# A graph layer with a sort on one core: the compare and exchange stage in six narrow instructions, turned weights in SBUF, and an eleventh gather slot

## The reference

```python
# x: 8192 x 512; src, dst: 131072 node numbers; edge_weight: 131072
h   = layernorm(x) @ L0_gnn_weight.T                    # 8192 x 512
x   = x + segment_sum(edge_weight[:, None] * h[dst], src, 8192)
y   = layernorm(x)
# small network on a few columns of y: nibbles of columns 64..112 by argmax(> 0.5),
# seven layers of 160 x 160, result rounded to 0..15, one-hot, times a mask
x   = x + (y + 2 * one_hots in columns 128..160)
```

## Time and profile before

| | |
|---|---|
| median of three runs | 1762.64 us (1757.96 to 1767.19) |
| profiled execution | 1770.79 us, its span 1768.9 us |
| TensorE (PE), busy | 1601.1 us, 91% |
| VectorE (DVE), busy | 1099.5 us, 62% |
| ScalarE (ACT), busy | 604.3 us, 34% |
| GpSimd (POOL), busy | 1093.6 us, 62% |
| granted TensorE clock | 0.978 of full speed over the span |

### The profile page before, as it was taken

The page is one execution under the profiler, slowest core; times in us unless marked ns, Lnnn a source line. Parts: engine busy times, 40 slices in busy tenths (PEclk is TensorE's granted clock), DMA queues, the critical chain, the costliest instruction groups (busy, mean ns, idle before and its releaser), DMA issues.

```text
span 1768.9 us, 28755 instructions
## 1 busy us (share of the span) xinstructions
PE 1601.1 (91%) x4076; PEld 661.9 (37%) x4077; DVE 1099.5 (62%) x4047; ACT 604.3 (34%) x1354; POOL 1093.6 (62%) x1114
## 2 busy tenths in 40 slices
PE   7999997999989989989998999999999999995995
PEld 4555543333333333333332333333333333332442
DVE  7666575667666876777668766767633333335465
ACT  7777632222222222222222222222234444443341
POOL 1000005777777777777777777777777777775930
PEclk9999998999999999999999999999999999997798
DMA  7333215777777777766776777777777777772334
GB/s 258 116 136 135 89 68 166 206 204 203 200 199 206 201 201 204 202 196 197 201 201 197 206 203 207 201 205 203 206 209 209 208 209 210 208 210 59 132 111 140
DMA packets 121761, 323.87 MB, mean 183 GB/s; under 512 B 20434, under 2 KB 39154, under 8 KB 121586
## 3 DMA queue, kind: packets, MB, share of 16 engines
q0 software_dynamic: 81920, 268.50, 53.4%
q1 hardware_dynamic: 39666, 53.48, 8.8%
HBM read 288.35 MB, written 33.55 MB: 182 GB/s over the span
## 4 chain that ended last, share of the span: by engine, by line
PE 51%; DMA 15%; DVE 13%; POOL 9%; issue 8%; DVEq 3%; ACT 1%; SPq 1%; ACTq 0%
PE psum L1220 30%; DMA region<-h_rows,region 14%; PE psum L1127 12%; POOL region L531 9%; PE psum L1299 4%; DVE region L937 3%; DVE region L846 2%; PE psum L1116 2%; DVEq L937 2%; DVE region L832 2%; DVE region L838 1%; DVE region L840 1%; DVE region L844 1%; PE psum L1267 1%; PE psum L1137 1%
## 5 line engine op out<-in xcount | busy, mean ns | idle before, releaser
L531 POOL DMA_INDIRECT region<-h_rows,region x1024 | 1013.0, 989 | 579.9 <-DMA h_rows<-region 268.1
L1220 PE MATMUL psum<-region 128*128 x2552 | 1204.9, 611 | 109.4 <-DVE region L937 56.3
L1220 PEld LDWEIGHTS psum<-region 128*128 128x128 f32 x2552 | 443.8, 189 | 832.2 <-issue 822.2
L937 DVE SCALAR_TENSOR_TENSOR region<-region 128x128 f32 (+1 forms) x1276 | 444.9, 351 | 388.3 <-PE psum L1220 269.2
L691 ACT ACTIVATE x<-psum 128x512 f32<-128x512 f32 x192 | 114.7, 597 | 772.5 <-PE psum L1220 772.5
L1127 PE MATMUL psum<-region 128*128 128x512 f32 x512 | 230.2, 593 | 0.9 <-ACT region L593 0.9
L846 DVE COPY_PREDICATED region<-region 128x256 f32<-128x256 int32 x407 | 179.5, 441 | 0.0
L674 ACT ACTIVATE psum<-x 128x512 f32<-128x512 f32 x256 | 153.7, 601 | 8.1
L832 DVE TENSOR_TENSOR region<-region 128x128 int32<-128x128 f32 x452 | 128.9, 285 | 24.9 <-ACT region L620 23.4
L844 DVE TENSOR_TENSOR region<-region 128x128 f32<-128x128 f32 x452 | 128.6, 285 | 0.0
L840 DVE TENSOR_TENSOR region<-region 128x128 f32<-128x128 f32 x452 | 128.2, 284 | 0.1
(11 more groups left out here) (151 smaller groups left out, 639.7 us busy)
## 6 DMA issues: line engine op xcount, KB each, us to landing
x<-in_x SPq DMA_DIRECT2D x16, 1024.0 KB, 5.6
h_rows<-region SPq DMA_DIRECT2D x64, 256.0 KB, 2.0
region<-h_rows,region POOLq DMA_INDIRECT x1024, 3.7
out<-x SPq DMA_DIRECT2D x4, 2816.0 KB, 10.8
out<-x SPq DMA_DIRECT2D x8, 640.0 KB, 3.4
region<-in_L_gnn_weight SPq DMA_DIRECT2D x1, 1024.0 KB, 5.5
region<-in_src SPq DMA_DIRECT2D x4, 128.0 KB, 2.3
region<-in_dst SPq DMA_DIRECT2D x4, 128.0 KB, 2.3
```

Source lines behind the costliest of these rows:

```text
L531: pool.indirect_dma_start(gathered[:, (c + 1) % RING, :], None, h_dram, bass.IndirectOffsetOnAxis(ap=dst_i[g][:, i:i + 1], axis=0),).then_ ...
L937: dve.scalar_tensor_tensor(spread[:, slot % SR, :], iota_n[:, bass.ds((tile - (g * T + 1)) * P, P)], src_f[g][:, bass.ds(chunk - (g * NC + ...
L1220: pe.matmul(banks[:, bass.ds(pe.snap(tile_wanted) % AGG, 1), :].rearrange("p t f -> p (t f)"), spread[:, slot % SR, :], gathered[:, bass.d ...
```

## The change

A stage now has six instructions, and weights are exchanged in place in `weight[g]`: compare (as before); copy the low half of the weights (128 columns) aside into `low_kept`; minima; predicated copy of the high weights into the low half; maxima; predicated copy of the kept weights into the high half. The second weight buffer is gone. In the slot "turned" VectorE now also copies the turned weights from PSUM to `weight[g]`, and waits for both copies. The pack slot loses its copy. TensorE waits for the copies before it turns again. The table of times and the shares in the plan get new values. The space that `other_weights` leaves lets RING go from 10 to 11.

```diff
-    RING = 10
+    RING = 11
-        vector_times = {"pack": 6.0, "flip": 0.3, "keys": 0.65, "weights": 0.65, "turned": 1.9, "maxima": 2.5,
+        vector_times = {"pack": 6.0, "flip": 0.3, "keys": 0.6, "weights": 0.85, "turned": 1.9, "maxima": 2.5,
-            return {"keys": 1.0, "weights": 0.9, "turned": 0.9, "flip": 0.4, "rest": 0.5}.get(what, 0.7)
+            return {"keys": 1.0, "weights": 1.0, "turned": 1.2, "flip": 0.4, "rest": 0.5}.get(what, 0.7)
-        AT_TAB = AT_SORT + 4 * NC
+        AT_TAB = AT_SORT + 3 * NC + NC // 2
...
-        SORT_STEPS = {"pack": 3, "flip": 1, "keys": 3, "weights": 2}
+        SORT_STEPS = {"pack": 2, "flip": 1, "keys": 3, "weights": 3}
...
                     elif what == "keys":
-                        low, high = pairs(keys_now, j)
+                        low, high = pairs(keys[now], j)
                         to_low, to_high = pairs(keys[1 - now], j)
+                        low_w, high_w = pairs(weight[g], j)
                         swap = single(swaps[half], j)
+                        kept = single(low_kept, j)
                         dve.wait_ge(s_sort[g], done - 1)
                         dve.tensor_tensor(swap, low, high, ALU.is_gt).then_inc(s_sort[g], 1)
-                        if turns > BY_SCALAR[g]:
-                            dve.wait_ge(s_turn_w[g], turns)
-                        elif turns:
+                        if turns:
                             dve.wait_ge(s_wgt_in[g], turns)
                         dve.wait_ge(s_sort[g], done)
-                        dve.tensor_copy(weights[1 - now], weights_now).then_inc(s_sort[g], 1)
+                        dve.tensor_copy(kept, low_w).then_inc(s_sort[g], 1)
                         dve.wait_ge(s_sort[g], done + 1)
                         dve.tensor_tensor(to_low, low, high, ALU.min).then_inc(s_sort[g], 1)
                         done += 3
                     elif what == "weights":
                         dve.wait_ge(s_sort[g], done - 1)
+                        dve.copy_predicated(low_w, swap, high_w).then_inc(s_sort[g], 1)
+                        dve.wait_ge(s_sort[g], done)
                         dve.tensor_tensor(to_high, low, high, ALU.max).then_inc(s_sort[g], 1)
-                        dve.wait_ge(s_sort[g], done)
-                        dve.copy_predicated(both(weights[1 - now], j),
-                                            swap.unsqueeze(2).to_broadcast(both(weights_now, j).shape),
-                                            both(weights_now, j)[:, :, ::-1, :]).then_inc(s_sort[g], 1)
-                        done += 2
+                        dve.wait_ge(s_sort[g], done + 1)
+                        dve.copy_predicated(high_w, swap, kept).then_inc(s_sort[g], 1)
+                        done += 3
...
                     elif what == "turned":
                         turns += 1
-                        if turns <= BY_SCALAR[g]:
-                            dve.wait_ge(s_key_in[g], turns)
-                        else:
-                            weights_now = turned_weights
+                        if turns > (TURNS, HEAD_TURNS, 0, 0)[g]:
                             dve.wait_ge(s_turn_k[g], turns)
-                            dve.tensor_copy(keys_now, turned_keys).then_inc(s_key_in[g], 1)
-                            dve.wait_ge(s_key_in[g], turns)
+                            dve.tensor_copy(keys[now], turned_keys).then_inc(s_key_in[g], 1)
+                            dve.wait_ge(s_turn_w[g], turns)
+                            dve.tensor_copy(weight[g], turned_weights).then_inc(s_wgt_in[g], 1)
+                        dve.wait_ge(s_key_in[g], turns)
...
                 pe.wait_ge(s_sort[g], steps - 1)
-                if 0 < turn <= BY_SCALAR[g]:
-                    pe.wait_ge(s_key_in[g], turn)
+                if turn or g:
+                    pe.wait_ge(s_key_in[g if turn else g - 1], turn if turn else TURNS)
```

More of the change, by code:

```diff
@@ L211, in gnn_ffn @@
         keys = [carve(NC), carve(NC)]
[L212 removed]
+        rest = carve(NC + NC // 2)
         swaps = [rest[:, i * NC // 2:(i + 1) * NC // 2].bitcast(I32) for i in range(2)]
[L214 to L215 removed]
+        low_kept = rest[:, NC:NC + NC // 2]
+        below = low_kept
         over = rest[0:T, 0:NSP]
@@ L621, in turn_out @@
                 act.wait_ge(s_turn_w[g], turn + 1)
-                act.activation(weights_of(g)[buffer], turned_weights, ACT.Copy).then_inc(s_wgt_in[g], 1)
+                act.activation(weight[g], turned_weights, ACT.Copy).then_inc(s_wgt_in[g], 1)
             def turns_out(n):
@@ L780, in sort_edges @@
                 done = turns = now = half = 0
-                weights = weights_of(g)
-                keys_now, weights_now = keys[0], weights[0]
-                def both(a, j):
-                    return a.rearrange("p (b s d) -> p b s d", s=2, d=1 << (j if j < 7 else j - 7))
                 def pairs(a, j):
-                    return both(a, j)[:, :, 0, :], both(a, j)[:, :, 1, :]
+                    v = a.rearrange("p (b s d) -> p b s d", s=2, d=1 << (j if j < 7 else j - 7))
+                    return v[:, :, 0, :], v[:, :, 1, :]
                 def single(a, j):
@@ L803, in sort_edges @@
                         dve.wait_ge(s_edge[g][2], 16)
-                        dve.tensor_copy(weights_now, weight[g]).then_inc(s_sort[g], 1)
-                        done += 3
+                        done += 2
                     elif what == "flip":
@@ L1139, in turn_edges @@
                 pe.wait_ge(s_sort[g], steps)
-                if 0 < turn <= BY_SCALAR[g]:
-                    pe.wait_ge(s_wgt_in[g], turn)
+                if turn or g:
+                    pe.wait_ge(s_wgt_in[g if turn else g - 1], turn if turn else TURNS)
                 for b in range(NC // P):
-                    last = pe.transpose(bank(WEIGHT_BANK)[:, b * P:(b + 1) * P],
-                                        weights_of(g)[buffer][:, b * P:(b + 1) * P], ident[:, :])
+                    last = pe.transpose(bank(WEIGHT_BANK)[:, b * P:(b + 1) * P], weight[g][:, b * P:(b + 1) * P], ident[:, :])
                 last.then_inc(s_turn_w[g], 1)
```

8 lines of the change are left out of this document (removed).

## The result

| | before | after |
|---|---|---|
| median | 1761.09 us (6 runs, 1757.96 to 1767.19) | 1773.01 us (6 runs, 1770.38 to 1777.78) |
| profiled execution | 1770.79 us, span 1768.9 | 1773.75 us, span 1772.0 |

The ratio is 1.0072, with a 95% interval of 1.0050 to 1.0093: the change made the kernel slower by 12 us. That is inside the range, and on the side that had 0.25. The profiled execution of before lies 9.7 us above its median, so the two traces show only 3 us of the 12. On two of the chips that the experiments ran on, the kernel before took some 240 us longer, and every kernel traced there spent them in the gather stage (1544 to 1558 us), so a ratio counts only against the kernel before on the same chip.

The account below looks back on a forecast made before the run. GpSimd's own pace, one gather after another without waiting for slots, was taken to bound the gather stage. The terms were 1762.6 - 1 (gathers) + 2 (stalls at sort starts) = 1764 us, range 1742 to 1784.

Parts of the forecast that it names:

- the side that had 0.25: Whole kernel: the outcome slower by more than 0.5% (8.8 us), given chance 0.25.
- The bound now: Gather stage: GpSimd never waits for a free slot; each gather takes 0.95 us plus its own 0.30 us gap.
- A narrow stage alone: Sorting on VectorE without builds: six instructions take 1.13 to 1.20 us where five took 1.14; 1.20 taken, +0.06.
- A stage with two builds: VectorE beside the gathers: a sort stage with two builds goes from 1.87 to 1.93 us, with 2.12 available.
- What VectorE can bear: Gather stage: VectorE's added work fits its waits of 3.7 us per turn; thinner reserve at sort starts, +2 us (0 to 5).
- C: Rival: VectorE becomes the bound if a stage with two builds exceeds 2.12 us; +18 us, 1780 us, chance 0.20.
- The gathers: GpSimd's gathers beside sorting: lengthening goes from 42 to 41 us, -1 us; -24 if no chain forms, +8 at most.
- A: Main case: no change, 1764 us (1755 to 1773), with 41 us of longer gathers left; chance 0.53.
- Rival B: Gathers: only the copies' running time lengthens them, so 42 us becomes 25, -17 us, 1746 us; chance 0.27.
- The turned copy, hidden: The 45 turns: the second copy from PSUM fits the 0.92 us gap before the next build; otherwise 15 us.
- The plan, zero: Nine sort stages move from the first stage to beside the gathers, 10 us more there; first stage zero, up to 2 us.
- The eleventh slot, zero: The gathers' ring: one more slot adds 1.25 us to a reserve that is never used up, so zero.

Follow-up runs that it names:

- both variants of before that ran on the first chip: The kernel before with only the plan's new times and shares (0.9994 of before), and with only the turned weights copied from PSUM to SBUF as well (0.9991).
- five narrow instructions: The kernel after with the second predicated copy left out, so half of the weights are not exchanged: 0.9976 of the kernel before.
- kernel before with registers ahead: The kernel before with a build's register work moved ahead of the last sort instructions and their wait: 0.9956 of before, then 0.9981 on another chip.

## Why the prediction was right and wrong, point by point

- **The bound now** (GpSimd's own pace): right for before. Its gaps of 0.30 us stay in both variants of before that ran on the first chip.
- **A narrow stage alone, 1.13 to 1.20 us, 1.20 taken**: 25.75 - 24.61 = 1.14 us, the lower end. The narrow copy has the pitch of 0.13 that the sign flips suggested.

```profile
24.61 0.28 DVE L823 TENSOR_TENSOR region<-region 128x128 int32<-128x128 f32 x1
24.81 0.22 DVE L827 COPY region<-region 128x128 f32<-128x128 f32 x1
24.94 0.28 DVE L829 TENSOR_TENSOR region<-region 128x128 f32<-128x128 f32 x1
...
25.55 0.29 DVE L837 COPY_PREDICATED region<-region 128x128 f32<-128x128 int32 x1
25.75 0.28 DVE L823 TENSOR_TENSOR region<-region 128x128 int32<-128x128 f32 x1
```

- **A stage with two builds, 1.93 us of 2.12: this step failed.** It measured 2.18 above, and 2.14 in the median of the 250 stages of that form: +0.27 us where I had +0.06. I added the difference of the stage alone to 1.87, as if a build cost the same behind any instruction, and wrote that "no stall is added by order alone", since no instruction waits for the one just ahead of it. It doesn't cost the same, and order adds a stall: waiting for the instruction two back is enough to hold up the register work of the build. The medians give for before 1.14 (the stage) + 2 x 0.27 (from a build to the next instruction) + 0.19 (register work that shows behind the minimum, 0.39 in place of 0.20) = 1.87. After it is 1.14 + 2 x 0.27 + 0.26 (behind the minimum, 0.46 in place of 0.20) + 0.20 (behind the second predicated copy, 0.40 in place of 0.20) = 2.14. Behind the predicated copy of before nothing showed, since that copy waits for the minimum and the register work was over in time; five narrow instructions have 0.20 there, with the same width as after. The other 0.07 are what the narrow plain copy should have saved: the build stands 0.79 us behind the comparison in both kernels. Before's profile could have warned me: 1.87 - 1.14 = 0.73 us in the earlier trace rows, where two builds alone account for 0.54.
- **What VectorE can bear.** The point from which C decides, 2.12 us, was right: at 2.14 the wait for the turn is gone (103.8 to 2.6 us), TensorE is at a lead of one, and GpSimd waits for slots from its gather 240 on. C was what happened, and I gave it 0.20. Its size, 18 us, was worked out for a stage of 2.4 us; 26 us of waits came at 2.14. The reserve of 3.7 us a turn, which I set against C, was an average that can't be carried about. VectorE waited 103.8 + 62.3 = 166 us before in the first 992 us of the gathers, and still waits 84.2 + 2.6 = 87; but that lies where it is ahead, and it may be 8 builds ahead at most, so nothing of it helps where it is behind.
- **The gathers, -1 us (-24 to +8): the second step that failed.** They measured -26. I reckoned with each line's mean excess and more chances to meet it; but the 0.37 us of a gather under the comparison isn't a property of that line. In after, 45 gathers start under it and have 0.03 each, since the chain of comparison, copy and minimum keeps a gather out only where VectorE's stream has no gap ahead of it. I reckoned 16.3 us for that term, and it measured 1.3. "If no chain forms, -24" was the bound, and it is what came.
- **The two failures cancel** in the profiled stage: the 26 us that gathers save are waited again. That is why a time about 0.5% above the predicted 1764 (1773.01, +9.0) comes from two steps that are both wrong by some 25 us. That the two are of one size is luck. The sum itself was A's; the mechanism was C's.
- **Rival B** (the copy's running time, 1746 us) is false in cause, though its 25 us of excess come closer than A's 41: with a copy of double width the excess stays at 12.8 to 15.8. With it falls, for this kernel, the rule of the Trainium skill (SBUF — State Buffer, "Who interferes with whom") as the whole account: with 452 wide copies between SBUF places gathers can be nearly as short as in after (12.8 and 15.8 us against 12.1), and with 407 of them, wide predicated copies and no gaps they are the longest (66.9 us). The comparison and the minimum, which have two inputs in SBUF and are no copies, each keep a gather out to their own end.
- **The turned copy, hidden**: right. It alone measures 0.9991, and in after the build follows the second copy by 0.58 us where 0.92 lay behind the only one. In both kernels the build stands 0.50 us behind the end of the keys' copy, for which the program waits, and the second copy runs meanwhile.
- **The plan, zero**: right in the kernel before (0.9994), wrong in after, where "10 us more later" met a VectorE with nothing to spare: 1.0053 with it and 1.0017 without. **The eleventh slot, zero**: right.

Why 12 us and not zero can be told only in part. Before's profiled run was a long one. As an estimate, which puts the whole of its 9.7 us into the gather stage, that stage would be near 1314 us in a median run (1761.1 less 277.4, 167.5 and 1.9 around the span), which at 1283 us for the undisturbed pace means some 32 us of longer gathers and not 42. After's gather stage at its median is 1323.1: 9 us more, and 3 us are in stage three (170.3 against 167.5), which no edit touches. So in a median run the gathers would gain about 17 us, and GpSimd waits 26. By parts, the plan together with the new stage is about 6 of the 12 (the two runs with and without it), and the narrow instructions with their builds the rest. That split rests on intervals that overlap.

No version is shown to beat both. The kernel before with registers ahead is the only one with a ratio clearly below 1 (0.9956, then 0.9981 with an interval to 1.0001), but both chips were of the kind with the long gather stage; on the first kind, where the gathers' length is what counts, its 25 us of longer gathers could well make it slower. It wasn't run there.

## What to carry to other kernels

Measure an instruction by its pitch at the place where it will stand. The register work of the next instruction can only begin once the wait ahead of it in the program is over: behind a wait for something that has just run it stands in the open, behind a wait that was over long ago it is hidden. So look at what the last instruction before it waits for, and not only at whether an instruction waits for its neighbour. When the engine beside the bound one is at 90% of what it can bear, count everything in its cycle, and treat "x us of y available" as the forecast's main risk. And when a stage is bound by one engine, what that engine gains is worth only as much as the slack of the next.

## What the runs showed of the hardware that was not expected

- Register work for one dynamically addressed build costs VectorE 0.33 us (151 + 93 + 88 ns), begins when the instruction before it is handed out, and with the steps between them the build can start 0.46 us after it has begun (after). If the last wait is over early, all of it is hidden, even behind a predicated copy of 128 columns: pitch to the build 0.20 us with five narrow instructions, 0.335 behind one of 256 in before. If that wait ends 0.06 us before the copy starts, the pitch behind one of 128 is 0.40 (after), and 0.20 again with the work done ahead of the wait.
- A predicated copy of 128 columns takes 0.28 us with a pitch of 0.20, one of 256 columns 0.43 or 0.44 with 0.33; but many of the narrow ones last 0.44 too (mean 348 to 350 ns of 452), and then the pitch to the next is 0.23. A plain fp32 copy of 128 columns has a pitch of 0.135 us, one of 256 columns 0.20.
- GpSimd's issue of an indirect DMA that begins under a comparison of two SBUF inputs is held to the comparison's end when VectorE's stream had a gap just ahead (211 of 211). Without the gap it is held to the end of the copy behind (128 columns, 56 of 68) or of the minimum behind that (copy of 256 columns, 140 of 152). Over 1024 gathers that and its like come to 12 to 67 us, with the same amount of data moved, and repeat within 4 us from chip to chip.
- The same kernel before took 1761 and 1768 us on some chips and 2001 and 2005 on others. In the kernel after, stages one and three had the same lengths (278.9 and 170.3 us), and the gather stage took 226 us more. Waits of after on such a chip, from the first gather to 1605 us:

```profile
POOL region L525 <- SPq L472: 270.4, 238, 3.4
...
POOL region L525 <- issue: 216.5, 635, 1.7
...
DVE region L829 <- DVE region L827: 11.2, 14, 1.2
```

  Even between two neighbours in VectorE's own program, where the trace of after on the first kind of chip has no idle time, 1.2 us can pass, and GpSimd has such stretches as well. Longer gathers and waits add up to 262 to 276 us in all eight kernels of these chips, whichever way they are divided, so something else sets the pace there. What it is stays open: the trace names no cause.
